# Attention and quantised FFN over 32 batches: one more batch step ordered by hand, an early layernorm, and weight unpacking in two halves

## The reference

```python
x = x + xattn(layernorm(x), ctx, Wq, Wk, Wv, Wskip)
x = x + ffn(layernorm(x), qweight, scales, zeros, bias)
# xattn: q = Wq @ x; k = Wk @ ctx; v = Wv @ ctx; energy = q^T k / sqrt(128)
#        out = Wskip @ x + v @ softmax(energy)^T
# ffn:   w = (interleave(qweight & 15, qweight >> 4 & 15) - round(zeros / scales)) * scales
#        y = x @ w + bias
```

## Time and profile before

| what | value |
|---|---|
| median of 3 runs | 517.02 us (516.99 to 517.34) |
| profiled execution | 517.71 us, of which the span of its instructions is 515.6 us |
| TensorE busy | 496.5 us, 96% |
| GpSimd busy | 467.1 us, 91% |
| VectorE busy | 435.3 us, 84% |
| ScalarE busy | 376.8 us, 73% |

### The profile page before, as it was taken

The page is one execution under the profiler, slowest core; times in us unless marked ns, Lnnn a source line. Parts: engine busy times, 40 slices in busy tenths (PEclk is TensorE's granted clock), DMA queues, the critical chain, the costliest instruction groups (busy, mean ns, idle before and its releaser), DMA issues.

```text
span 515.6 us, 9359 instructions
## 1 busy us (share of the span) xinstructions
PE 496.5 (96%) x2672; PEld 299.4 (58%) x2672; DVE 435.3 (84%) x1001; ACT 376.8 (73%) x867; POOL 467.1 (91%) x711
## 2 busy tenths in 40 slices
PE   4888999999999999999999999999999999999987
PEld 3544456665666656566665566666556666565644
DVE  4989898888988888898888889888889888887752
ACT  4889778777787777778777777877777877777520
POOL 4786999999999999999999999999999999999763
PEclk9999999999999999999999999999999999999999
DMA  8774678778968987887878786787767687757653
GB/s 305 204 156 108 183 176 157 204 187 187 197 171 202 156 199 183 196 182 179 211 150 193 185 206 176 180 204 156 196 178 197 172 202 190 168 130 145 167 130 120
DMA packets 227203, 92.65 MB, mean 180 GB/s; under 512 B 209488, under 2 KB 214352, under 8 KB 227152
## 3 DMA queue, kind: packets, MB, share of 16 engines
q1 hardware_dynamic: 226432, 91.91, 73.9%
q10 hardware_dynamic: 720, 0.14, 0.2%
HBM read 23.87 MB, written 16.78 MB: 79 GB/s over the span
## 4 chain that ended last, share of the span: by engine, by line
PE 83%; POOL 8%; issue 3%; DVE 3%; ACT 2%; DMA 1%; POOLq 0%; ACTq 0%; SPq 0%
PE ps_y L1020 38%; PE ps_e L974 15%; PE ps_o L1015 13%; PE ps_o L1009 7%; PE ps_kv L992 2%; PE ps_y L1026 2%; PE ps_kv L988 2%; POOL sb_prob L273 2%; POOL sb_xn_lo L318 2%; PE ps_e L970 1%; POOL sb_o L267 1%; DMA sb_x<-in_x_dram 1%; ACT sb_prob L506 1%; POOL sb_rstd L281 1%; DVE sb_neg_max L697 1%
## 5 line engine op out<-in xcount | busy, mean ns | idle before, releaser
L1020 PE MATMUL ps_y<-sb_wf,sb_xnt_hi 128*128 128x512 f16 x496 | 188.3, 380 | 3.3 <-DMA sb_xnt_lo<-sb_xn_lo 3.3
L1020 PE MATMUL ps_y<-sb_wf,sb_xnt_lo 128*128 128x512 f16 x496 | 188.0, 379 | 0.0
L506 ACT ACTIVATE sb_prob<-ps_e,sb_neg_max 128x256 f32<-128x256 f32 x256 | 118.2, 470 | 51.5 <-DVE sb_neg_max L697 51.4
L273 POOL TENSOR_SCALAR sb_prob<-sb_prob,sb_rsum 128x256 f32<-128x256 f32 x256 | 122.5, 492 | 7.3 <-DVE sb_rsum L702 7.2
L706 DVE TENSOR_TENSOR sb_p_lo<-sb_prob,sb_p_hi 128x1024 f16<-128x1024 f32 x64 | 78.1, 1220 | 36.5 <-ACT sb_p_hi L515 36.4
L267 POOL TENSOR_TENSOR sb_o<-sb_prod,sb_x 128x512 f32<-128x512 f32 x63 | 84.9, 1348 | 5.8 <-DVE sb_prod L740 5.8
L697 DVE TENSOR_REDUCE sb_neg_max<-ps_e 128x2 f32<-128x512 f32 x128 | 85.0, 682 | 1.8 <-PE ps_e L970 1.4
L515 ACT ACTIVATE sb_p_hi<-sb_prob 128x1024 f16<-128x1024 f32 x64 | 67.4, 1053 | 23.3 <-issue 23.3
L1020 PEld LDWEIGHTS ps_y<-sb_wf,sb_xnt_hi 128*128 128x128 f16 x496 | 48.4, 98 | 61.0 <-DMA sb_xnt_lo<-sb_xn_lo 4.3
L1020 PEld LDWEIGHTS ps_y<-sb_wf,sb_xnt_lo 128*128 128x128 f16 x496 | 48.5, 98 | 54.8
L974 PE MATMUL ps_e<-sb_k_hi,sb_xc_hi 128*128 128x256 f32 x224 | 78.6, 351 | 0.1
(11 more groups left out here) (150 smaller groups left out, 976.0 us busy)
## 6 DMA issues: line engine op xcount, KB each, us to landing
sb_x<-in_x_dram SPq DMA_DIRECT2D x32, 512.0 KB, 3.9
out_dram<-sb_o SPq DMA_DIRECT2D x63, 256.0 KB, 2.4
sb_ctx<-in_ctx_dram SPq DMA_DIRECT2D x32, 128.0 KB, 2.7
sb_q<-in_L_ffn_qweight_dram SPq DMA_DIRECT2D x4, 512.0 KB, 7.5
sb_pt_hi<-sb_p_hi SPq DMA_TRANSPOSE x64, 3.0
sb_pt_lo<-sb_p_lo SPq DMA_TRANSPOSE x64, 2.9
sb_scale_row<-in_L_ffn_scales_dram SPq DMA_DIRECT2D x1, 512.0 KB, 9.6
sb_xnt_hi<-sb_xn_hi SPq DMA_TRANSPOSE x32, 2.8
```

The lines of the kernel that those rows point to most:

```text
L273: last = pool.tensor_scalar(prob[:, b % 2, j, t, :], prob[:, b % 2, j, t, :], rsum[:, j, t:t + 1], P_SCALE, ALU.mult, ALU.mult)
L506: done = act.activation(prob[:, b % 2, j, t, :], ps_e[j % 2][:, t, :], ACT.Exp, bias=neg_max[:, j, t:t + 1], accum_out=esum[:, j, t:t + 1])
L1020: pe.matmul(ps_y[h][:, :], xnt_p[s][:, q % 2, kt, :], wf[:, kt, h * HALF:(h + 1) * HALF], start=kt == 0 and s == 0, stop=False)
```

## The change

Batch 3's step is taken out of the general steps on ScalarE and VectorE and written out in their run-in lists; there `run_steps` now starts at 4. GpSimd, TensorE and SP keep the general step 3. In the run-in lists these things move as well:

- ScalarE: `unpack` is two functions. Low and high halves of a block stand apart, between the exponentials of batch 2. The layernorm of batch 0 and its high part come ahead of the first exponentials of batch 2. The first exponentials of batch 3 come between `apply_norm2(1)` and `xn_high(1)`.
- The high half of the last block goes to GpSimd (`unpack_last_high`), with a semaphore of its own on which TensorE waits for the eighth block.
- GpSimd: `zero_point_sign` comes behind the first two normalisations of batch 2; `inverse_std1(3)` ahead of `inverse_std2(1)`; `split_row_sum(1)` ahead of `inverse_std1(4)`.
- VectorE: the residual and statistics of batch 1, half 0, come ahead of the third row maximum of batch 2; the nibbles of block 3 come earlier.
- TensorE: `attend(1, 1)` comes ahead of `scores(2, 3)`, and `skip(1, 1)` with `keys_values(3)` ahead of `scores(2, 2)`.

```diff
+            def unpack_last_high():
+                pool.wait_ge(nib_done, QT)
+                pool.tensor_scalar(wf[:, 2 * QT - 1, :], q_sb[:, QT - 1, :], 1.0 / XN_SCALE, None,
+                                   ALU.mult).then_inc(last_wf_done, 1)
...
                 inverse_std2(0)
-                zero_point_sign()
                 split_row_sum(0)
                 xn_low(0)
                 normalise(2, 0)
                 normalise(2, 1)
+                zero_point_sign()
                 seed_sources()
+                unpack_last_high()
+                inverse_std1(3)
                 inverse_std2(1)
                 normalise(2, 2)
                 normalise(2, 3)
-                inverse_std1(3)
+                split_row_sum(1)
                 inverse_std1(4)
-                split_row_sum(1)
                 xn_low(1)
...
-            def unpack(k):
+            def unpack_low(k):
                 act.wait_ge(nib_done, k + 1)
-                act.activation(wf[:, 2 * k, :], nib_sb[:, k % 2, :], ACT.Copy, scale=1.0 / XN_SCALE)
+                ins = act.activation(wf[:, 2 * k, :], nib_sb[:, k % 2, :], ACT.Copy, scale=1.0 / XN_SCALE)
+                if k == QT - 1:
+                    ins.then_inc(wf_done, 1)
+
+            def unpack_high(k):
                 act.activation(wf[:, 2 * k + 1, :], q_sb[:, k, :], ACT.Copy,
                                scale=1.0 / XN_SCALE).then_inc(wf_done, 1)
...
-                unpack(0)
-                exps(2, 0)
+                unpack_low(0)
                 apply_norm2(0)
                 xn_high(0)
+                exps(2, 0)
                 exps(2, 1)
+                unpack_high(0)
                 exps(2, 2)
+                unpack_low(1)
+                unpack_high(1)
                 exps(2, 3)
-                unpack(1)
-                unpack(2)
+                unpack_low(2)
+                unpack_high(2)
                 probs_hi(2, 0)
-                unpack(3)
+                unpack_low(3)
                 centre(3)
                 keys_hi(3)
                 values_hi(3)
                 probs_hi(2, 1)
                 apply_norm2(1)
+                exps(3, 0)
                 xn_high(1)
+                centre(4)
+                keys_hi(4)
+                values_hi(4)
+                exps(3, 1)
+                centred_hi(4)
+                exps(3, 2)
+                probs_hi(3, 0)
+                exps(3, 3)
+                key_projection_hi()
+                context_hi(5)
+                apply_norm2(2)
+                probs_hi(3, 1)
+                xn_high(2)
...
+                residual(1, 0)
+                stats2(1, 0)
                 row_max(2, 2)
                 invert(2, 0)
                 invert(2, 1)
-                residual(1, 0)
-                stats2(1, 0)
-                row_max(2, 3)
                 low_nibbles(2)
                 high_nibbles(2)
                 residual(1, 1)
+                row_max(2, 3)
                 stats2(1, 1)
                 aggregate2(1)
+                low_nibbles(3)
+                high_nibbles(3)
                 invert(2, 2)
                 invert(2, 3)
                 stats1(3, 0)
                 stats1(3, 1)
                 aggregate1(3)
                 variance1(3)
-                low_nibbles(3)
-                high_nibbles(3)
                 seed_rows()
                 value_scale(3)
+                probs_lo(2, 0)
                 context_max(4)
-                probs_lo(2, 0)
                 values_lo(3)
                 stats1(4, 0)
+                row_max(3, 0)
                 stats1(4, 1)
                 aggregate1(4)
                 variance1(4)
                 probs_lo(2, 1)
                 scale_product(0, 0)
+                scale_product(0, 1)
+                value_scale(4)
+                row_max(3, 1)
+                invert(3, 0)
+                residual(2, 0)
+                row_max(3, 2)
+                stats2(2, 0)
+                stats1(5, 0)
+                stats1(5, 1)
+                aggregate1(5)
+                invert(3, 1)
+                variance1(5)
+                keys_lo(4)
+                values_lo(4)
...
                     if kt % 2 == 0:
                         pe.wait_ge(wf_done, kt // 2 + 1)
+                    if kt == KT - 1:
+                        pe.wait_ge(last_wf_done, 1)
...
-                scores(2, 2)
                 skip(1, 1)
                 keys_values(3)
+                scores(2, 2)
+                attend(1, 1)
                 scores(2, 3)
-                attend(1, 1)
                 first_ffn()
```

More of the change, by code:

```diff
@@ L121, in xattn_ffn_program @@
         khi_done, klo_done = sem("khi"), sem("klo")
-        nib_done, wf_done, zp_step = sem("nib_done"), sem("wf_done"), sem("zp_step")
+        nib_done, wf_done, last_wf_done, zp_step = sem("nib_done"), sem("wf_done"), sem("last_wf"), sem("zp_step")
         src_done, rows_turned, rows_done, seed_made = sem("src"), sem("rows_turned"), sem("rows"), sem("seed_made")
@@ L610, in _ @@
             run_in()
-            run_steps(step, 3)
+            run_steps(step, 4)
         @block.vector
@@ L867, in run_in @@
                 scale_product(0, 0)
+                scale_product(0, 1)
[12 more added lines that the diff above has]
+                values_lo(4)
+                invert(3, 2)
+                residual(2, 1)
+                row_max(3, 3)
+                stats2(2, 1)
+                aggregate2(2)
+                invert(3, 3)
+                probs_lo(3, 0)
+                context_max(5)
+                scale_product(1, 0)
+                key_projection_lo()
+                context_lo(5)
+                probs_lo(3, 1)
             def step(t):
```

## The result

The changed kernel takes 519.36 us (median of 6 runs, 518.29 to 520.49) against 517.03 for the kernel before: ratio 1.0042, 95% interval 1.0032 to 1.0053, so 2.33 us slower (1.65 to 2.74). Forecast were 518.1 and a range that ends at 519.0: the direction was right, the size too small by half. Its profiled execution took 520.49 us, of which the span is 518.5.

What follows compares the result with a forecast made beforehand. GpSimd's chain was taken to bound the kernel before about 76 us: normalisations ending at 51.0 plus ScalarE's 4.3 put batch 1's low half at 55.3 instead of 54.2, so +1.1 us, 518.1; range 515.4 to 519.0.

Steps and rivals of the forecast that it cites:

- What bounds: Up to about 76 us: GpSimd's chain sets the start of batch 1's low half, and that sets the end.
- S: Start on GpSimd of the low half of batch 1's second layernorm: 54.20 before, forecast 55.3, 1.1 us late.
- Early layernorm and nibbles: Batch 0's layernorm ahead of exponentials: 1.60 us early, 0.8 lost to VectorE's nibbles holding GpSimd; net 0.8 early.
- The unpacking: Last block's high half on GpSimd: 1.84 us, priced from four normalisations, bounds 1.0 and 2.3.
- The reciprocal deviation: Batch 3's, moved ahead of batch 2's last two normalisations: 0.55 us more; ScalarE and VectorE have it in time.
- The new meeting: VectorE's low probabilities of batch 2, half 0, hold GpSimd at bias and normalisations: 1.0 us, bounds 0 and 1.15.
- The sum for the normalisations: End of batch 2's normalisations on GpSimd: 47.36 - 0.80 + 1.04 + 1.84 + 0.55 + 1.00 = 51.0.
- ScalarE's tail: From batch 2's normalisations to batch 1's low half: 3.35 us of ScalarE work, 0.91 for batch 3's exponentials, 0.04 semaphore; 4.3.
- The sign step: Four small GpSimd steps moved from a free gap to behind two normalisations of batch 2: 1.04 us on the path.

Runs made afterwards that it cites:

- 7: Kernel before with only the last high half unpacked on GpSimd, batch 3's reciprocal deviation issued ahead of it; 519.43 us, ratio 1.0046.
- 9: Kernel before plus ten multiplies at the end of GpSimd's list, to time each form; one multiply of 1024 elements 2.8 us, two constants 1.09.
- 13: Kernel before plus twelve instructions at the end of GpSimd's list, to time more forms; int32 to float16 with two operations 1.20 us.
- 12: Changed kernel with GpSimd's unpacking in the two-operation form, a second multiply by 1.0; 517.84 us, ratio 1.0011.
- 11: Changed kernel with batch 3's reciprocal deviation ahead of the unpacking on GpSimd; 519.02 us, ratio 1.0048.
- 1: Changed kernel with the high half of the last weight block unpacked on ScalarE again; 517.57 us, ratio 1.0011.
- 14: Changed kernel with two-operation unpacking behind batch 3's reciprocal, batch 2's last scores and row maximum and batch 3's statistics moved earlier; 517.36 us, ratio 1.0007.
- 2: Changed kernel with batch 3's first exponentials behind the high half of batch 1's layernorm; 518.58 us, ratio 1.0025.
- 16: As 10, with the sign step back in GpSimd's gap ahead of batch 0's row sum; 516.70 us, ratio 0.9986.
- 17: As 14, with the sign step back in GpSimd's gap ahead of batch 0's row sum; 517.25 us, ratio 1.0002.
- 3: Changed kernel with the four sign steps back ahead of batch 0's row sum; 519.11 us, ratio 1.0040.
- run 0: The changed kernel timed and profiled again, no edit; 519.55 us, ratio 1.0048.
- 10: Changed kernel, unpacking on ScalarE, batch 3's step generic, batch 2's last scores and row maximum and batch 3's statistics moved earlier; 516.42 us, ratio 0.9987.
- 4: Kernel before with only the last block's high half unpacked on GpSimd, behind the seed sources; 520.88 us, ratio 1.0066.
- 15: As 4, with the unpacking in the two-operation form; 519.36 us, ratio 1.0044.

## Why the prediction was wrong in size

**What bounds.** Right, and the firmest part: GpSimd sets S, S sets the end, nothing behind 76 us matters. S moved by 1.56 and F by 1.59. Not said, and shown by 7: batch 3's exponentials are a second path to F, which can come last where TensorE's clock falls behind its wait for them. In the change TensorE waits only 0.18 and 0.53 us for them.

**Early layernorm and nibbles.** Right. With the start-up's 1.18 taken off, the layernorm is at 32.16 (forecast 32.17), and the first FFN starts at 40.67 (forecast 40.8); the nibbles held the row sum's steps (0.69 and 0.54 for 0.19) and later the seed's. The seed rows end at R + 18.11, forecast R + 18.3.

**The unpacking: the step that failed.** It was put at 1.84, bounds 1.0 to 2.3; it took 2.75 to the next start. That is 0.91 of GpSimd's path, and the upper bound itself was too low. With 2.75 in its place the forecast's own sum gives 519.0, the end of its range. I priced by element count and by the number of inputs; the form with one operation is what costs, as 9, 13 and 12 show. My estimate from the Trainium skill (GPSIMD Engine Reference, "Elementwise — side-by-side cycle accounting"), 1.54, was too low as well.

**The reciprocal deviation.** Its 0.57 stands as forecast (0.55). That ScalarE and VectorE would have it in time was wrong: they waited 0.80 and 1.07 us for it. It cost nothing (11).

**The new meeting.** Forecast a hold of 1.0; the bias step took 0.96 for 0.26, so 0.70. In 1, 12 and 14 the same meeting falls on the normalisations and costs about 1.0.

**The sum for the normalisations** was R + 24.5 (51.0); they end at R + 24.8 (52.49): +0.91 for the unpacking, -0.30 for the hold, -0.20 at the seeds and -0.1 in small steps. That the sum came within 0.3 is luck: terms put too high hid two thirds of the unpacking's error.

**ScalarE's tail.** 4.40 (52.49 to 56.89), forecast 4.3. ScalarE's idle of 2.26 and TensorE's of 1.18 are there as forecast. Its term of 0.91 for the exponentials is too high: without them (2) S comes only 0.3 to 0.7 earlier, as GpSimd has the row sum and a reciprocal to do meanwhile.

**The sign step.** Its 1.04 on the path is real in GpSimd's list (1.1 measured). Removing it buys nothing in 16 and 17, where another chain is as late; in the change itself 3 leaves that open, as its profile has the fallen clock. A sum along one chain says what is added to it; for what is taken away the next chain has to be known too. The prediction followed one chain and never put a time on the second, over the transposed block and VectorE's nibbles.

**The rest.** In the first profile S gives 1.56 of the 2.33 us, in the second 1.93, with F 2.14 late, since the transposed block landed later. So some executions of the change lose more than GpSimd's list alone says, over the second chain. How often is not measured: only two of twelve were profiled. The start isn't the cause of the median, as run 0 showed, and for the clock no cost in the median is shown. 1.93 lies within the interval of the 2.33 (1.65 to 2.74), 1.56 just below it; the cause of what is left stays open.

## What to carry to other kernels

Price an instruction by a row of the very same form (operation count, operands), not by its element count; where there is none, measure a pair of it at the end of a list. Before work is put in front of another engine's input, ask what follows that input: an idle stretch that ends on a value which goes back to one's own earlier result is a round trip, no slack. And where a second chain is about as late, an undoing shows less than its term; the gain of 10 came from taking a variance out from behind a late residual. Last, look at the granted clock of the very stretch before a profile's wait is put down to an edit (3), and at a second profile of the same kernel (0).

## What the runs showed of the hardware

- GpSimd's multiply of a tile by one constant takes 2.8 us for 1024 elements per partition, by two constants 1.09, and a plain copy 1.07. The Trainium skill (GPSIMD Engine Reference, "Elementwise — side-by-side cycle accounting") gives 1.8 cycles per element as the best case of a tight loop, 769 ns for 512, and 1.03 cycles per element for its smallest bodies. The runs here show both a dearer form (1.54 us for 512) and a cheaper one (1.09 for 1024).
- A form's cost doesn't depend much on whether int32 or float32 is read and float16 or float32 written: 2.81 to 2.91, and 1.09 to 1.20.
- TensorE's granted clock fell to its lower level behind a wait in the profiles of 0 (wait of 1.16 us, at 61.97), 3 (2.07, at 38.85), 4 (2.38, at 52.49) and 7 (2.49, at 57.22), and not in the change's first one (1.18, at 62.13). The mean clock of the run is 0.997 or less in all six runs of 4 and all five of 7, in seven of twelve of the change, and in none of the five of 15, whose waits are several short ones (0.77, 0.55, 0.30, 0.88).
- What the fall costs depends on where it lies: about 1.2 us on the chain to the last nibbles in 3, and at most 0.2 us between S and F in 0.
- A transposed block of the same kernel landed 1.0 us later in one execution than in another, measured from R (12.81 against 11.78).
